# A pipelined transformer layer in which every engine gets its work in another order: one gate chunk, one value chunk and the next input in other places

## The reference, cut to what matters

```python
for i in range(DEPTH):                       # 6
    x = attn_layer(shift_tokens(x), Wqkv[i], q_scale[i], k_scale[i], Wo[i]) + x
    x = ffn_layer(shift_tokens(x), ln_g[i], ln_b[i], W1[i], b1[i], W2[i], b2[i]) + x
# attn_layer: q, k, v = split(x @ Wqkv); q = l2norm(q)*qs; k = l2norm(k)*ksc; rotary with scale;
#   local attention: windows of 32 queries see their own and the window before; softmax; @ Wo
# ffn_layer: xn = layernorm(x)*g + b; a, gate = split(xn @ W1 + b1); (a * gelu(gate)) @ W2 + b2
# ffn width 341: chunks of 128, 128 and 85 rows
x = layernorm(x + ...)
```

## Time and profile before

| | |
|---|---|
| time, median of 3 runs | 3797.65 us (3793.39 to 3800.12) |
| time of the profiled execution | 3798.59 us |
| its span | 3796.8 us |
| TensorE clock granted, mean | 0.986 of full speed |
| PE busy | 3597.4 us (95%) |
| PE weight loads busy | 3062.5 us (81%) |
| ScalarE busy | 3368.7 us (89%) |
| VectorE busy | 3121.7 us (82%) |
| GpSimd busy | 2747.9 us (72%) |
| DMA, mean | 35 GB/s |

### The profile page before, as it was taken

How to read it: one execution, slowest core, us unless ns; L and a number is a source line. 1 busy time by engine, 2 the same in 40 slices (tenths; PEclk the granted TensorE clock), 3 DMA queues, 4 the chain that set the end, 5 groups by cost and what they waited for, 6 DMA issues and landing times.

```text
span 3796.8 us, 133054 instructions
## 1 busy us (share of the span) xinstructions
PE 3597.4 (95%) x47336; PEld 3062.5 (81%) x47336; DVE 3121.7 (82%) x6999; ACT 3368.7 (89%) x10923; POOL 2747.9 (72%) x2058
## 2 busy tenths in 40 slices
PE   7989979999999999999999999999999999999996
PEld 4666668888888888888888888888888888888885
DVE  7888878887888888888888888888788888878884
ACT  7888859999999999999999999999999999998894
POOL 0111159888888888888788888888888887888772
PEclk9999989999999999999999999999999999999998
DMA  2000001111111111111111111111111111111111
GB/s 97 7 11 11 7 23 48 33 33 30 40 48 35 36 29 35 42 42 39 29 36 37 39 44 34 31 31 44 42 39 32 33 36 39 36 28 37 40 34 31
DMA packets 165627, 132.97 MB, mean 35 GB/s; under 512 B 114929, under 2 KB 125553, under 8 KB 164721
## 3 DMA queue, kind: packets, MB, share of 16 engines
q1 hardware_dynamic: 164976, 124.45, 13.3%
HBM read 25.84 MB, written 4.19 MB: 8 GB/s over the span
## 4 chain that ended last, share of the span: by engine, by line
PE 73%; DVE 5%; issue 4%; ACT 3%; SPq 1%; DMA 0%; DVEq 0%; POOL 0%; POOLq 0%; ACTq 0%
PE bank L974 10%; PE bank L928 10%; PE bank L954 8%; PE bank L1013 8%; PE bank L996 6%; PE bank L893 4%; PE bank L894 4%; PE bank L895 4%; PE bank L867 4%; PE bank L989 3%; PE bank L851 2%; PE bank L853 2%; PE bank L852 2%; PE bank L907 2%; PE bank L905 2%
## 5 line engine op out<-in xcount | busy, mean ns | idle before, releaser
L1210 POOL TENSOR_TENSOR a_rn<-a_ssqc,a_minus_half 128x16 f32<-128x16 f32 x384 | 1113.2, 2899 | 536.4 <-DVE a_ssqc L1381 531.0
L1156 ACT ACTIVATE a_E<-bank,a_negmax 128x96 f32<-128x96 f32 x3072 | 1012.7, 362 | 31.8 <-DVE a_negmax L1330 31.0
L1232 POOL TENSOR_TENSOR a_r<-a_u,a_rn 128x512 f32<-128x512 f32 x768 | 789.2, 1047 | 0.6
L1219 POOL TENSOR_TENSOR a_PN<-a_E,a_erec 128x384 f32<-128x384 f32 x768 | 742.2, 986 | 13.8 <-DVE a_erec L1389 13.6
L1156 ACT ACTIVATION_READ_ACCUMULATOR a_E<-bank,a_negmax 128x1 f32 x3072 | 705.4, 230 | 0.0
L1138 ACT ACTIVATE a_QK<-bank 128x512 f32<-128x512 f32 x768 | 466.7, 608 | 152.0 <-PE bank L928 151.9
L1343 DVE TENSOR_TENSOR a_u<-bank,a_rot_c 128x512 f32<-128x512 f32 x768 | 522.3, 680 | 2.4 <-ACT a_sq L1130 2.4
L1353 DVE TENSOR_TENSOR a_v<-bank,a_rot_s 128x512 f32<-128x512 f32 x768 | 523.1, 681 | 0.0
L1130 ACT ACTIVATE a_sq<-bank 128x512 f32<-128x512 f32 x768 | 481.9, 627 | 44.2 <-PE bank L895 13.0
L1114 ACT ACTIVATE a_PT<-bank 128x512 f32<-128x512 f32 x768 | 485.1, 632 | 24.0 <-PE bank L954 20.4
L928 PE MATMUL bank<-ident,a_r 128*128 128x128 f32 x3072 | 483.7, 280 | 17.8 <-DVE a_bias L1315 11.8
(11 more groups left out here) (140 smaller groups left out, 8445.8 us busy)
## 6 DMA issues: line engine op xcount, KB each, us to landing
a_V_even<-a_V_odd SPq DMA_DIRECT2D x384, 128.0 KB, 2.3
a_V_even<-a_V_odd SPq DMA_DIRECT2D x192, 64.0 KB, 2.3
a_raw<-in_qkv SPq DMA_DIRECT2D x20, 384.0 KB, 3.6
a_x_sh<-X SPq DMA_DIRECT2D x48, 128.0 KB
a_V_even<-a_V_odd SPq DMA_DIRECT2D x192, 32.0 KB, 2.0
a_f_sh<-X SPq DMA_DIRECT2D x48, 128.0 KB
a_x_sh<-X SPq DMA_DIRECT2D x48, 127.0 KB
a_f_sh<-X SPq DMA_DIRECT2D x48, 127.0 KB
```

The lines of the kernel that those rows point to most:

```text
L1156: ins = act.activation(E[:, s.par, k, :], p_s[:, i % 2, col:col + KW], ACT.Exp, bias=negmax[:, s.par, k:k + 1], accum_out=esum[:, s.par, k ...
L1210: pool.tensor_tensor(rn[:, a.par, :], ssqc[:, a.par, :], minus_half[:, :], ALU.pow).then_inc(S["rn"], 1)
L1219: pool.tensor_tensor(PN[:, s.par, 2 * hp:2 * hp + 2, :].rearrange("p i (b k) -> p i b k", b=2)[:, :, :, 0:KW], spread(E[:, s.par, half, :] ...
L1232: pool.tensor_tensor(heads(r[:, a.par, half]), heads(u[:, a.par, half]), rn[:, a.par, mm * 2 * HG:(mm + 1) * 2 * HG].unsqueeze(2).to_broad ...
```

## The change

The same instructions, semaphores and buffers stay, in another order in the `cycle` of each engine. Three pieces of the feed-forward's and input's work change place on TensorE: gate chunk 0 goes from the middle of step 3 (bank p_tb) to behind `values` (bank p_ta); gate chunk 1 goes in step 4 from behind `project(1)` to ahead of it; the transposes of the next x go in step 7 from behind `transpose_qk(0)` to ahead of it. The waits in `transpose_qk` and `transpose_probs` for the emptied gate bank follow the bank. ScalarE's exponentials of the first half are parted: two come right behind `queries_and_keys(0)`, two behind `queries_and_keys(1)`. `squares(0)` goes ahead of `outputs`. On VectorE `add` goes ahead of `reciprocals(1)`, `cosines(1)` ahead of `norms`, `stats` and the layer-change work forward, and `residual` from the head of step 7 into step 6.

```diff
@@ TensorE @@
             def cycle(n, p):
...
                 logits(n, p)
-                transpose_qk(n, p, 0)
-                if p == P_BIAS:
-                    shifts(n)
-                if p == P_GATE and n < NI:
-                    up(n, p, 0, 0, p_tb)
                 if p == P_X and n + 1 < NI:
                     transpose_x(n + 1)
+                transpose_qk(n, p, 0)
+                if p == P_BIAS and feed:
+                    shifts(n)
+                if p == P_GATES and feed:
+                    up(n, p, 1, 0, p_tb)
                 project(n, p, 1)
...
-                if p == P_GATES and n < NI:
-                    up(n, p, 1, 0, p_tb)
...
                 values(n, p)
+                if p == P_GATE and feed:
+                    up(n, p, 0, 0, p_ta)
...
@@ ScalarE @@
             def cycle(n, p):
+                feed = n < NI
                 probs(n, p, 1)
+                squares(n, p, 0)
                 outputs(n, p)
-                squares(n, p, 0)
-                queries_and_keys(n, p, 0)
-                if p == P_GATE and n < NI:
-                    gate_out(n, 0, p_tb)
                 if p == P_X and n + 1 < NI:
                     high_x(n + 1)
+                queries_and_keys(n, p, 0)
+                exps(n, p, 0, 0)
+                if p == P_TURN and feed:
+                    turned(n)
+                if p == P_GATES and feed:
+                    gate_out(n, 1, p_tb)
                 squares(n, p, 1)
-                if p == P_TURN and n < NI:
-                    turned(n)
-                if p == P_GATES and n < NI:
-                    gate_out(n, 1, p_tb)
-                exps(n, p, 0, 0)
-                exps(n, p, 0, 1)
-                if p == P_GATES and n < NI:
+                values(n, p)
+                if p == P_GATE and feed:
+                    gate_out(n, 0, p_ta)
+                if p == P_GATES and feed:
                     gate_out(n, 2, p_ta)
                 queries_and_keys(n, p, 1)
-                values(n, p)
+                exps(n, p, 0, 1)
                 probs(n, p, 0)
...
@@ GpSimd @@
             def cycle(n, p):
+                probs(n, p, 0)
                 power(n, p)
-                probs(n, p, 0)
                 probs(n, p, 1)
+                units(n, p, 0)
                 units(n, p, 1)
-                units(n, p, 0)
...
@@ VectorE @@
             def cycle(n, p):
-                if p == P_X:
-                    residual(n)
+                feed = n < NI
                 maxima(n, p)
-                if p == P_VALUES and n < NI:
+                cosines(n, p, 0)
+                if p == P_TURN and feed:
+                    turned(n)
+                if p == P_VALUES and feed:
                     product(n, 0, p_tb)
                 if p == P_X and n + 1 < NI:
                     low_x(n + 1)
-                cosines(n, p, 0)
-                if p == P_TURN and n < NI:
-                    turned(n)
-                if p == P_VALUES and n < NI:
+                sines(n, p, 0)
+                if p == 0:
+                    stats(n)
+                if p == P_BIAS and feed:
+                    split_up(n)
+                    biases(n)
+                if p == P_VALUES and feed:
                     product(n, 1, p_ta)
                 if p == P_X:
                     product(n, 2, p_ta)
-                sines(n, p, 0)
+                cosines(n, p, 1)
                 norms(n, p)
-                if p == P_BIAS and n < NI:
-                    split_up(n)
-                    biases(n)
-                cosines(n, p, 1)
+                if p == P_VALUES and feed:
+                    residual(n)
+                reciprocals(n, p, 0)
+                sines(n, p, 1)
                 clamp(n, p)
-                sines(n, p, 1)
+                add(n, p)
                 if p == P_NORM:
                     norm(n)
-                reciprocals(n, p, 0)
-                if p == 0:
-                    stats(n)
...
                 reciprocals(n, p, 1)
-                add(n, p)
```

More of the change, by code:

```diff
@@ L918, in transpose_qk @@
                     if mm == 1:
-                        if p in (P_GATE, P_GATES):
-                            ge(pe, S["gate"], NF * f + 1 + (p == P_GATES) if f >= 0 else 0)
+                        if p == P_GATES:
+                            ge(pe, S["gate"], NF * f + 2 if f >= 0 else 0)
                         if p == P_VALUES:
@@ L943, in transpose_probs @@
                             ge(pe, S["f_xl"], f + 1)
+                        if p == P_GATE:
+                            ge(pe, S["gate"], NF * f + 1 if f >= 0 else 0)
                         if p == P_GATES:
@@ L1161, in cycle @@
             def cycle(n, p):
+                feed = n < NI
                 probs(n, p, 1)
+                squares(n, p, 0)
                 outputs(n, p)
-                squares(n, p, 0)
-                queries_and_keys(n, p, 0)
-                if p == P_GATE and n < NI:
-                    gate_out(n, 0, p_tb)
                 if p == P_X and n + 1 < NI:
                     high_x(n + 1)
-                squares(n, p, 1)
-                if p == P_TURN and n < NI:
-                    turned(n)
-                if p == P_GATES and n < NI:
-                    gate_out(n, 1, p_tb)
-                exps(n, p, 0, 0)
-                exps(n, p, 0, 1)
-                if p == P_GATES and n < NI:
+                queries_and_keys(n, p, 0)
[4 more added lines that the diff above has]
+                    gate_out(n, 1, p_tb)
+                squares(n, p, 1)
+                values(n, p)
+                if p == P_GATE and feed:
+                    gate_out(n, 0, p_ta)
+                if p == P_GATES and feed:
                     gate_out(n, 2, p_ta)
                 queries_and_keys(n, p, 1)
-                values(n, p)
+                exps(n, p, 0, 1)
                 probs(n, p, 0)
@@ L1424, in cycle @@
                     product(n, 2, p_ta)
-                sines(n, p, 0)
+                cosines(n, p, 1)
                 norms(n, p)
-                if p == P_BIAS and n < NI:
-                    split_up(n)
-                    biases(n)
-                cosines(n, p, 1)
+                if p == P_VALUES and feed:
+                    residual(n)
+                reciprocals(n, p, 0)
+                sines(n, p, 1)
                 clamp(n, p)
-                sines(n, p, 1)
+                add(n, p)
                 if p == P_NORM:
                     norm(n)
-                reciprocals(n, p, 0)
-                if p == 0:
-                    stats(n)
-                if p == (P_GELU if n < NI else 0):
+                if p == (P_GELU if feed else 0):
                     feed_forward_out(n)
```

## The result

The changed kernel is slower: 3850.74 us (median of 4, 3847.91 to 3854.36) against 3798.81 us of the kernel before beside it, ratio 1.014 (95% interval 1.0123 to 1.0156). The forecast was 3757 with a range of 3735 to 3788, and 0.86 for faster: wrong in sign, by 94 us. The profiled span is 3849.6 us.

A forecast was written before the change was run, and what follows sets the result against it. TensorE was taken to bound the kernel, its waits (2.25 us of a 65.67 us iteration) being all an order can win. 3798.6 - 23.5 (ordinary iterations) - 1 (iteration 1) - 9 - 4 - 4 gave 3757, range 3735 to 3788.

The forecast's parts named there:

- The loop of the masks: Steps 1 to 4: exponentials ahead of `squares(1)` shorten ScalarE's loop from 7.11 to 6.92 us; minus 0.38 us an iteration.
- the gate chunks: Step 4: the 128-row chunk is emptied sooner, cutting TensorE's wait for the 85-row chunk by 0.23 of 0.33 us.
- `down`: Step 5: TensorE's wait for the copy of half 1, now ahead of two exponentials, goes; minus 0.20 us.
- step 7: Next x: the 85-row value chunk waits for the copy of `queries_and_keys(0)`; a loss of 0.30 us an iteration.
- The -4 at n % 8 = 7: Layer-change iterations: shorter waits for the low part of x (by 0.3) and at `down` (about 0.5); minus 4 us.
- The -4 at the end: Kernel's end: `last_stats` waits less for a DMA because ScalarE's `values` is earlier; 1.3 us three times, minus 4 us.
- The biases: Iterations with n % 8 = 4: biases come 1.7 us sooner, ahead of `cosines(1)` and `norms`; 1.8 us five times, minus 9.
- The failed step: GpSimd's new order, on an engine covered 83% of the time, was to cost 0, ends plus and minus 0.1 us.
- The failed step beneath it: VectorE: with `add` moved, only the reciprocal stands before `maxima`, leaving about 1.0 us free a step ahead of it.
- Rival F: GpSimd and VectorE block each other, `add` held to the end of `power` every step: plus 384, 4180 us; chance 0.01.
- rival D: VectorE is late: late `maxima` holds ScalarE's queue, plus 1.4 us an iteration, 3845 us; chance 0.05.
- The free 1.0 us: VectorE, uncovered 17% of the time, was taken to have about 1.0 us free in a step, ahead of `maxima`.

The follow-up runs named there:

- the fastest kernel: The changed kernel with VectorE's and GpSimd's orders of before, plus `split_up` and `biases` ahead of `norms` on VectorE: 3767.56 us, ratio 0.9926.

## Why the prediction was wrong

- **The loop of the masks, the gate chunks, `down`, step 7.** Forecast -0.14, -0.09 and -0.14 for the masks in steps 1, 3 and 4, -0.23 and -0.20 for chunk and `down`, +0.30 for step 7: -0.50. Measured outside step 2: -0.57. These terms held. With old orders on VectorE and GpSimd an ordinary iteration is 0.52 us shorter, forecast 0.51, but the equal sum is partly luck: step 2 grew by 0.29, the others gave more. That kernel gained 11 us, and with the biases 29.
- **The -4 at n % 8 = 7** didn't come: with old orders on VectorE and GpSimd these five iterations together take 2.0 us more than before, where the forecast had 6.6 less (4 and five times 0.51). The -4 at the end stays open. Iterations 44 to 46 took 5 us less, but this sum also differs by 8 us between the fastest kernel and the one with `transpose_x` back, whose ordinary iterations are equal; and the stretch ahead of iteration 0, which no edit touches, differs by 7 us between executions.
- **The biases.** Forecast -9 us for the five; the waits fell from 11.8 to 5.3 us, -6.5. Under VectorE's and GpSimd's old orders they were worth 18 (3785.73 to 3767.56): the two profiled executions, 25 us apart, show 9.8 in the five and 1.7 in iteration 0, which has biases too. So they are worth 10 to 12 us, near the forecast; the rest lies in the two stretches just named.
- **The failed step: GpSimd, "its new order starts with what is ready first; r is used only two steps later: 0", ends plus and minus 0.1.** The free 17% of the earlier trace rows were read as slack in every step. The kernel before, by steps 0, 1 and 2 (columns as in the earlier trace rows):

```profile
1960.45:1967.38 6.93, 6.93 (x112) 6.27 (x110) 6.86 (x12) 6.18 (x24) 5.58 (x5) 1.00 0.18 42
1967.38:1974.51 7.13, 7.01 (x112) 6.29 (x110) 7.05 (x20) 6.70 (x25) 7.02 (x7) 1.00 0.14 31
1974.51:1982.33 7.82, 7.62 (x115) 6.60 (x114) 7.13 (x16) 7.28 (x26) 7.82 (x7) 1.00 0.21 48
```

  GpSimd is free for 0.1 us in step 1 and not at all in step 2; its free time lies in other steps. The new order hangs `power` on `reciprocals(0)`, and the step's end feeds `deviation` and so `norm`, neither of which the sum had; with VectorE's old order it costs 108 us.
- **The failed step beneath it: `add` ahead of `reciprocals(1)`** was valued for what it frees ahead of `maxima`. That it comes to start just ahead of `power`, and `clamp` later, had no term.
- **Rival F (0.01)** named the mechanism, and "the trace disagrees" was the error. The earlier trace rows show `power` first and `add` inside it; but that is only one of the two cases, and the change was about to turn the order round. The case `add` first did stand in the trace of before, on another instruction, 194 times:

```profile
1970.55 1.22 DVE L1361 TENSOR_TENSOR a_u<-a_u,a_v 128x1024 f32<-128x1024 f32 x1
1971.43 1.82 POOL L1219 TENSOR_TENSOR a_PN<-a_E,a_erec 128x384 f32<-128x384 f32 x2
```

  (Kernel before, step 1 of iteration 22.) Two `probs` in a row take 1.6 us undisturbed, by their 0.82 each, and 1.82 here: the first is held for 0.2 of the 0.34 us in which `add` still runs. Over the whole trace the held ones last 1.43 us in the median. F's own figure, 4180, assumed that every step loses 1 us; only step 2 does, and there 2.55.
- **`stats` and `norm`, rival D.** Late `norm` and `maxima` are what TensorE feels, as D had it (3845, and 3850.74 was measured). The nearness of the number is luck. The free 1.0 us that D and the sum count isn't there: in the rows above VectorE is free for 0.07 us in step 0 and 0.08 in step 1. And most of the lateness is no work of `stats` and `norm` passing through, which D counts, but instructions held and a wait for the root (to which early `stats` adds, through the late `clamp`).

The Trainium skill (SBUF — State Buffer, Who interferes with whom) calls the shared ports of VectorE and GpSimd an exclusive lock, and says, of VectorE's two-port modes, that whoever issues first has them for the whole instruction. The traces here bear out the half that matters: `add` first, 287 of 287 `power` calls held; `units` first, `add` held (1.75 us for 1.21). They disagree on one case: `power` first, with 16 columns in and out and 2.90 us long, did not hold `add` in any of 293 overlaps.

## What to carry to other kernels

Before you move an instruction on one engine, list what runs on the engine that can hold it, and who starts first by how much; a lead of 0.06 us cost `power` 1.03 us here, so an order is only safe with a margin, or with an instruction between (here `sines(1)` between `clamp` and `add`). An engine that is 83% busy on average may have no slack at all in some steps: read its free time step by step, not as a mean. A late engine can also hold another one without any wait in the profile; then only the durations show it. And when a trace seems to refute a rule, check that it shows the rule's condition, not its mirror image.

## What the runs showed that was not expected

The hold has a size that follows from the overlap: `power` lasts 3.81 us when `add` leads by 0.17, 3.93 when it leads by 0.06, 2.90 when it trails; `deviation` 1.00 or 2.06. For the held ones the extra time is what was left of `add`, less 0.14 us, in nearly all of them. And the two new orders don't add up. VectorE's by GpSimd's orders give 3785.73 (old, old), 3838.12 (new, old), 3893.86 (old, new) and 3850.74 (new, new); the sum of the two single losses, 52 and 108 us, would be 160, and 65 were measured.
